# The up product of a batched LoRA kernel: float32 in 16-row, 64-column places of the array instead of float32r with split operands

## What is computed

```python
B_sel = B[adapter_ids]
A_sel = A[adapter_ids]
Bx = jnp.einsum('bni,bri->bnr', x, B_sel)
out = jnp.einsum('bnr,bor->bno', Bx, A_sel)
return x + out * SCALING
```

## Time and profile before

| | |
|---|---|
| median of 3 runs | 93.18 us (93.02 to 94.08) |
| profiled execution | 93.05 us |
| its span, first to last instruction | 91.3 us |
| TensorE busy | 79.9 us (88%) |
| VectorE, ScalarE, GpSimd busy | 59.6, 59.4, 64.1 us |
| DMA | 34.82 MB, mean 381 GB/s |
| granted TensorE clock, mean | 0.953 |

### The profile page before, as it was taken

The page is one execution under the profiler, slowest core; times in us unless marked ns, Lnnn a source line. Parts: engine busy times, 40 slices in busy tenths (PEclk is TensorE's granted clock), DMA queues, the critical chain, the costliest instruction groups (busy, mean ns, idle before and its releaser), DMA issues.

```text
span 91.3 us, 3632 instructions
## 1 busy us (share of the span) xinstructions
PE 79.9 (88%) x1466; PEld 63.2 (69%) x1466; DVE 59.6 (65%) x108; ACT 59.4 (65%) x155; POOL 64.1 (70%) x140
## 2 busy tenths in 40 slices
PE   3997899999999999999999999999999999563500
PEld 3996798877878778686878786878787877422100
DVE  0069541128695969696969696877768596998810
ACT  1356877996969596877869696969696959131000
POOL 6048955999897979797979788797979793810000
PEclk9999999999999999999999999999999999996555
DMA  0999999999999999999999999999999999989692
GB/s 20 314 381 413 406 408 413 404 408 413 400 408 413 400 409 409 406 406 404 409 417 404 417 417 409 415 413 411 417 413 411 417 413 415 386 321 377 275 384 88
DMA packets 10193, 34.82 MB, mean 381 GB/s; under 512 B 834, under 2 KB 1858, under 8 KB 10178
## 3 DMA queue, kind: packets, MB, share of 16 engines
q1 hardware_dynamic: 10032, 34.08, 93.8%
q10 hardware_dynamic: 146, 0.52, 1.5%
HBM read 17.83 MB, written 16.78 MB: 379 GB/s over the span
## 4 chain that ended last, share of the span: by engine, by line
PE 77%; DVE 6%; DMA 5%; ACT 2%; POOL 2%; DVEq 1%; issue 1%; POOLq 0%
PE t_bank L227 35%; PE bx_bank L238 19%; PE y_banks L258 19%; DMA x_all<-in_A 5%; PE y_banks L217 4%; DVE x_all L373 4%; POOL x_all L174 2%; DVE bx_parts L364 2%; DVEq L44 1%; ACT bx_parts L289 1%; ACT a_table L312 1%; ACT x_t L307 1%; DVE x_all L349 0%; POOLq L173 0%
## 5 line engine op out<-in xcount | busy, mean ns | idle before, releaser
L373 DVE TENSOR_TENSOR x_all<-y_banks,x_all 128x1024 f32<-128x1024 f32 x32 | 39.1, 1224 | 15.0 <-PE y_banks L258 14.5
L307 ACT COPY x_t<-t_bank 128x512 f32<-128x512 f32 x64 | 34.4, 590 | 12.1 <-PE t_bank L227 11.5
L166 POOL CAST a_duo<-a_table 128x512 fp32r x64 | 36.8, 617 | 3.7 <-ACT a_table L312 2.0
L227 PE MATMUL t_bank<-ident,x_all 128*128 128x128 f32 x256 | 34.9, 279 | 0.4 <-ACT x_t L307 0.4
L227 PEld LDWEIGHTS t_bank<-ident,x_all 128*128 128x128 f32 x256 | 27.5, 141 | 6.9 <-issue 5.3
L156 POOL COPY b_duo<-b_table 128x256 f32 x64 | 22.9, 403 | 7.8 <-PE bx_bank L238 7.8
L258 PE MATMUL y_banks<-a_duo,bx_parts 64*128 64x512 f32 x128 | 20.2, 434 | 3.3 <-ACT bx_parts L289 3.2
L238 PE MATMUL bx_bank<-x_t,b_duo 128*32 128x64 f32 x1024 | 20.7, 222 | 0.0
L238 PEld LDWEIGHTS bx_bank<-x_t,b_duo 128*32 128x32 f32 x1024 | 15.7, 109 | 5.4 <-issue 5.2
L364 DVE TENSOR_TENSOR bx_parts<-bx_bank,bx_parts 32x64 fp32r<-32x64 f32 x64 | 14.1, 220 | 4.8 <-ACT bx_parts L322 3.7
L258 PEld LDWEIGHTS y_banks<-a_duo,bx_parts 64*128 64x128 f32 x128 | 11.2, 192 | 7.0 <-issue 3.8
(11 more groups left out here) (12 smaller groups left out, 10.5 us busy)
## 6 DMA issues: line engine op xcount, KB each, us to landing
out_y<-x_all SPq DMA_DIRECT2D x32, 512.0 KB, 13.0
x_all<-in_x SPq DMA_DIRECT2D x15, 1024.0 KB, 19.1
x_all<-in_x SPq DMA_DIRECT2D x2, 512.0 KB, 6.1
x_all<-in_B ACTq DMA_DIRECT2D x1, 512.0 KB, 4.3
x_all<-in_A SPq DMA_DIRECT2D x2, 256.0 KB, 4.8
id_row<-in_ids ACTq DMA_DIRECT2D x1, 0.2 KB
```

Source lines behind the costliest of these rows:

```text
L166: last = nc.gpsimd.tensor_copy(a_duo[duo % 2][:, k, :], a_table[:, bass.ds(adapters[k] * BANK, BANK)])
L227: last = nc.tensor.transpose(t_bank[unit % 2][:, c * P:(c + 1) * P], x_all[:, 2 * duo + tile, at:at + P], ident[:, :])
L307: nc.scalar.copy(x_t[duo % 2][:, half * HALF:(half + 1) * HALF, tile, :], t_bank[unit % 2][:, :].rearrange("p (c n) -> p c n", c=HALF)).th ...
L373: nc.vector.tensor_tensor(here, product, here, ALU.add).then_inc(y_drained, 1)
```

## The change

- Up is float32, and nothing is split. Each of a duo's eight matmuls (two tiles, two sequences s, two halves h) has its own place: 16 rows in row group 2 x tile + h, 64 columns s. Nothing is accumulated: each writes its 64 tokens by 512 outputs alone.
- bx_bank's four quadrants hold a sequence's Bx each, 16 rows of 32. ScalarE copies them as they stand (128x64, L288), and each to the quadrant of the other half of the same tile (four copies of 16x64, L292). VectorE has no part in it, and does only the adds.
- B is gathered once (128 columns); A's table has each rank group at each quadrant.
- A is copied by VectorE alone, two copies of each group of adapters (L313), into a zeroed place; ScalarE's and GpSimd's parts in it go. VectorE copies six adapters to a_table, ScalarE two.
- Output halves are now even and odd columns pairs of a row of A (o as p, j, h), so the add steps through x by two.
- B's transposes go to bx_bank; transposes of x and of A are interleaved in another order at the start; 21 warm-up transposes.

```diff
-    A_BY_ACT = (1, 3, 5, 7)
-    A_BY_DVE = (0, 2, 4, 6)
-    WARM_UPS = 18
+    A_BY_ACT = (5, 7)
+    A_BY_DVE = (0, 1, 2, 3, 4, 6)
+    WARM_UPS = 21
...
-        b_duo = [sb(f"b_duo{i}", [P, DUO_SEQS, CHUNKS, QUAD]) for i in range(2)]
-        bx_parts = [sb(f"bx_parts{i}", [P, DUO_SEQS, P], F32R) for i in range(2)]
-        a_duo = [sb(f"a_duo{i}", [P, DUO_SEQS, BANK], F32R) for i in range(2)]
+        b_duo = [sb(f"b_duo{i}", [P, DUO_SEQS, CHUNKS, RANK]) for i in range(2)]
+        bx_sides = [sb(f"bx_sides{i}", [P, PER_TILE, SEQ]) for i in range(2)]
+        a_duo = [sb(f"a_duo{i}", [P, DUO_SEQS, BANK]) for i in range(2)]
...
-            for i in range(2):
-                nc.gpsimd.memset(bx_parts[i][:, :, :].bitcast(F32), 0.0).then_inc(parts_zeroed, 1)
+            nc.gpsimd.memset(a_copies[:, 0:GROUP, :, :], 0.0).then_inc(copies_zeroed, 1)
...
-                        last = nc.tensor.matmul(bx_bank[duo % 2][k * QUAD:(k + 1) * QUAD, 0:SEQ],
+                        last = nc.tensor.matmul(bx_bank[duo % 2][k * QUAD:k * QUAD + RANK, 0:SEQ],
...
-                            ranks = slice(h * K_UP, (h + 1) * K_UP)
-                            k = tile * PER_TILE + s
-                            last = nc.tensor.matmul(y_banks[tile][:, h * BANK:(h + 1) * BANK],
-                                                    bx_parts[duo % 2][ranks, k, :], a_duo[duo % 2][ranks, k, :],
-                                                    start=(s == 0), stop=(s == PER_TILE - 1))
+                            ranks = slice((2 * tile + h) * QUAD, (2 * tile + h) * QUAD + RANK)
+                            last = nc.tensor.matmul(y_banks[tile][s * SEQ:(s + 1) * SEQ, h * BANK:(h + 1) * BANK],
+                                                    bx_sides[duo % 2][ranks, int(s != h), :],
+                                                    a_duo[duo % 2][ranks, tile * PER_TILE + s, :],
+                                                    start=True, stop=True)
...
+                nc.scalar.copy(bx_sides[duo % 2][:, 0, :], bx_bank[duo % 2][:, 0:SEQ])
+                for tile in range(2):
+                    for s in range(PER_TILE):
+                        at, to = (2 * tile + s) * QUAD, (2 * tile + 1 - s) * QUAD
+                        last = nc.scalar.copy(bx_sides[duo % 2][to:to + RANK, 1, :],
+                                              bx_bank[duo % 2][at:at + RANK, 0:SEQ])
+                last.then_inc(bx_copied, 1)
...
+            nc.vector.memset(a_copies[:, GROUP:ADAPTERS, :, :], 0.0).then_inc(copies_zeroed, 1)
+            dve.wait_ge(copies_zeroed, 2)
             for g in range(2):
                 dve.wait_ge(a_loaded[g], 16)
-                for h in range(HALVES):
-                    nc.vector.tensor_copy(a_rounded(g, h, 0, 0), a_raw(g, h)).then_inc(a_high_dve, 1)
-                for h in range(HALVES):
-                    dve.wait_ge(a_high_dve, HALVES * g + h + 1)
-                    nc.vector.tensor_tensor(a_rounded(g, h, 0, 1), a_raw(g, h), a_part(g, h, 0, 0),
-                                            ALU.subtract).then_inc(a_rest_dve, 1)
+                for t in range(2):
+                    last = nc.vector.tensor_copy(a_copy(g, t), a_raw(g))
+                last.then_inc(a_copied, 1)
...
-                here = x_all[:, 2 * duo + tile, :].rearrange("n (p h j) -> n p h j", h=HALVES, j=J)
+                here = x_all[:, 2 * duo + tile, :].rearrange("n (p j h) -> n p h j", h=HALVES, j=J)
...
-            split_rest(0)
-            for duo in range(1, DUOS):
-                add_x(duo - 1, 0)
-                split_rest(duo)
-                add_x(duo - 1, 1)
-            add_x(DUOS - 1, 0)
-            add_x(DUOS - 1, 1)
+            for duo in range(DUOS):
+                for tile in range(2):
+                    add_x(duo, tile)
```

More of the change, by code:

```diff
@@ L9, in lora_kernel @@
 def lora_kernel(nc: bass.Bass, x: bass.AP, ids: bass.AP, a_in: bass.AP, b_in: bass.AP, out: bass.AP):
-    F32, F32R, I32 = mybir.dt.float32, mybir.dt.float32r, mybir.dt.int32
+    F32, I32 = mybir.dt.float32, mybir.dt.int32
     ALU = mybir.AluOpType
@@ L102, in a_bank, with a_raw, a_copy @@
             return y_banks[a % 2][:, half * BANK:(half + 1) * BANK]
[L104 to L111, removed]
+        def a_raw(g):
+            return (a_nat[:, g * GROUP:(g + 1) * GROUP, :]
+                    .rearrange("p a (j h r) -> p (a j) h r", h=HALVES, r=RANK))
+        def a_copy(g, t):
+            return (a_copies[:, g * GROUP:(g + 1) * GROUP, :, :]
+                    .rearrange("p a j (t h e r) -> p (a j) t h e r", t=2, h=HALVES, e=2)[:, :, t, :, 0, :])
         def a_row(a):
             return a_table[:, a * BANK:(a + 1) * BANK]
[L116 to L119, removed]
         @block.sync
@@ L198, in _ @@
                 for c in range(HALF):
-                    last = nc.tensor.transpose(t_bank[unit][:, c * P:(c + 1) * P],
+                    last = nc.tensor.transpose(bx_bank[unit][:, c * P:(c + 1) * P],
                                                b_nat[:, (unit * HALF + c) * P:(unit * HALF + c + 1) * P], ident[:, :])
@@ L223, in transpose_unit @@
                     pe.wait_ge(x_loaded[LOAD_OF[2 * duo + tile]], 16)
-                pe.wait_ge(t_copied, B_UNITS + UNITS * duo + unit - 1)
+                if duo or unit >= 2:
+                    pe.wait_ge(t_copied, B_UNITS + UNITS * duo + unit - 1)
                 for c in range(HALF):
@@ L264, in _ @@
                 a_unit(a)
[L265 to L268, removed]
+            transpose_unit(0, 0)
+            transpose_unit(0, 1)
+            a_unit(A_BANKS)
+            a_unit(A_BANKS + 1)
+            transpose_unit(0, 2)
+            transpose_unit(0, 3)
+            a_unit(A_BANKS + 2)
+            a_unit(A_BANKS + 3)
             for duo in range(DUOS):
@@ L311, in copy_a, with copy_bx @@
                 act.wait_ge(a_filled, a + 1)
-                nc.scalar.copy(a_row(a), a_bank(a)).then_inc(a_copied_act, 1)
-            def split_high(duo):
+                nc.scalar.copy(a_row(a), a_bank(a)).then_inc(a_table_act, 1)
+            def copy_bx(duo):
                 act.wait_ge(bx_done, duo + 1)
-                if duo < 2:
-                    act.wait_ge(parts_zeroed, duo + 1)
-                else:
+                if duo >= 2:
                     act.wait_ge(y_filled, 2 * (duo - 1))
-                for k in range(DUO_SEQS):
-                    s = k % PER_TILE
-                    last = nc.scalar.copy(bx_parts[duo % 2][0:QUAD, k, s * SEQ:(s + 1) * SEQ],
-                                          bx_bank[duo % 2][k * QUAD:(k + 1) * QUAD, 0:SEQ])
-                last.then_inc(high_done, 1)
@@ L342, in _ @@
[L342 removed]
+                    for unit in range(UNITS):
+                        copy_x(duo + 1, unit)
+                copy_bx(duo)
         @block.vector
         def _(dve):
+            nc.vector.memset(a_copies[:, GROUP:ADAPTERS, :, :], 0.0).then_inc(copies_zeroed, 1)
+            dve.wait_ge(copies_zeroed, 2)
             for g in range(2):
                 dve.wait_ge(a_loaded[g], 16)
[L348 to L353 removed]
+                for t in range(2):
+                    last = nc.vector.tensor_copy(a_copy(g, t), a_raw(g))
+                last.then_inc(a_copied, 1)
@@ L355, in _ @@
             for a in A_BY_DVE:
                 dve.wait_ge(a_filled, a + 1)
[L357 to L367 removed]
+                nc.vector.tensor_copy(a_row(a), a_bank(a)).then_inc(a_table_dve, 1)
```

102 lines of the change are left out of this document (28 added, 74 removed).

## The result

The changed kernel takes 94.81 us (median of 4 runs, 94.58 to 95.02) against 93.24 for the kernel before: ratio 1.018, 95% interval 1.015 to 1.020. It is slower, by more than the 1% that the prediction took as its bound; 91.0 was forecast, with a range of 89.8 to 94.8. Its profiled execution took 94.59 us for a span of 92.8.

The account below looks back on a forecast made before the run. TensorE and DMA were both read as nearly full, with compute setting the end. Span 91.3 us, -0.6 start, 0 periods, -2.0 end, +0.4 clock, +0.1 DMA: 89.2; with 1.75 around it, 91.0 us forecast, range 89.8 to 94.8.

Parts of the forecast that it names:

- TensorE waits for nothing: Mid-kernel chain before the change: TensorE alone, 4.32 to 4.34 us a duo, with no waiting.
- Up: Up in each duo: all eight float32 places run together, 1.12 us as before, bounds 1.05 and 1.35.
- Rivals 1, 2 and 3: Up slower: uneven starts 93.5 us (0.10); places partly blocked about 103 or 110 us (0.14); strict order 136 us (0.04).
- So the period stays 4.34 us.: Mid-kernel duos: copies and adds stay covered by TensorE, so 14 periods change the span by 0.
- rival 1: Up: places run but starts or weight loads are uneven, up 1.3 us, time 93.5 us; chance 0.10.
- Start and end: Loop begins 0.6 us earlier, near 13.1; at the end six adds take 7.5 us instead of 9.5, saving 2.0.
- a wait that I had ruled out: ScalarE's five small copies after down: 1.03 us, forecast as covered by some 0.5 us, so TensorE wouldn't wait.
- The floor: End of the span: remaining DMA traffic at 410 GB/s keeps the span from going under 88.4 us.
- Rival 4: End: stores fall behind and the DMA hides the gain, 91.5 us; chance 0.72 together with the forecast.

Follow-up runs that it names:

- runs 1 to 4: Changed kernel with 17 warm-up transposes and 2, 6, 12 or 18 small matmuls ahead of the work: 94.95, 95.37, 96.68 and 96.20 us.
- few_stores: Changed kernel storing only the first 128 of each tile's 1024 output columns: 90.66 us, ratio 0.975 to the kernel before.
- before_pad16: Kernel before with down's first four matmuls done twice in every duo, 192 instructions instead of 176: 97.54 us, ratio 1.050.
- down_half: Changed kernel with down over every second chunk only, 128 TensorE instructions in a duo instead of 192: 91.54 us, ratio 0.983 to the kernel before.
- s0: Changed kernel with 4 warm-up transposes fewer and 2 small float32 matmuls more ahead of the work: 94.95 us, ratio 1.021 to the kernel before.
- s16: As s0 but 6 small matmuls instead of 2, 16 instructions more ahead: 95.37 us, ratio 1.024 to the kernel before.
- s40: As s0 but 12 small matmuls instead of 2, 40 instructions more ahead: 96.68 us, ratio 1.035 to the kernel before.
- packets2k: Changed kernel with every load of x and every store cut into two of 2 KB per row: 97.71 us, ratio 1.050 to the kernel before.
- up_bf16: Changed kernel with up's operands (a_table, bx_sides, a_duo) in bfloat16, 176 instructions in a duo: 92.88 us, ratio 0.998 to the kernel before.
- s64: As s0 but 18 small matmuls instead of 2, 64 instructions more ahead: 96.20 us (93.55 to 97.22), too spread for a ratio.

## Why the prediction was wrong

**What bounded the kernel.** "TensorE waits for nothing" was read rightly from the earlier trace rows, but not how near it stood to a limit that no row of a busy engine shows. At 176 instructions a duo a block of 256 lasts 6.3 us, which is what the fetch needs under a full DMA. The kernel before was at its TensorE limit, within 2% of its DMA limit (91.3 against 89.8 us) and almost at its fetch limit together.

**Up.** Right in mechanism and size: 1.12 forecast, 1.04 measured. All eight places run at once: eight instructions start together, and the other eight 0.43 us later; that is 512 columns at two cycles, the price taken from the earlier trace rows. The second halves wait and the next places go on past them. The stops show that the program does have them product by product: before the one at 24.00 six products ran alone, with six starts and 0.45 us later six more, and behind it the other two did the same. The rule of strict program order (the Trainium skill, "TensorE: Matmul & The Clock Gate", packing small matmuls) would have given 4.1 us here; the trace doesn't agree with it. Rivals 1, 2 and 3 didn't happen.

**The failed step.** "So the period stays 4.34 us." I priced an operation by its time on the array, and never counted it as instructions, though I noted that a float32 product is two: up went from 16 to 32 instructions for each duo, all of TensorE's from 176 to 192. So the wait that I had at nothing, that for the program itself, cost 7.2 us: 4.1 in the stops and the split ups, 3.1 by the clock behind two of them. Undisturbed duos take 4.23 us, 0.11 less than forecast, worth 1.4 us over the 13 periods from the first up to the 14th; with the stops the mean period is 4.79. The stops are shown to be the fetch by three things: they keep their place in the program when the work is shifted (runs 1 to 4), go when the DMA is idle (few_stores), and appear in the old kernel at the new instruction count (before_pad16). That 94.81 lies so near the range's end is luck: its upper part stood for rival 1, an up of 1.3 us, which did not happen.

**Start and end.** The start was mis-sized. The 13.67 us of the earlier trace rows is the second duo's first transposes, where the loop begins in the program; the same transposes began at 12.01 us in the changed kernel, 1.7 us earlier, not 0.6 (13.1 forecast):

```profile
6.77 1.91 PE L192 MATMUL y_banks<-ident,x_all 128*128 128x128 f32 x16
...
12.01 1.04 PE L203 MATMUL t_bank<-ident,x_all 128*128 128x128 f32 x8
```

The 48 transposes from A on took the forecast 5.2 us, but A began at 6.77 instead of 7.9: B's eight took 1.04 us, not 1.91, since the clock had risen at 5.7 us (before, at 7.6). In the other runs of the changed kernel's kind it rose at 4.3 to 6.4 us, so part of this gain is that execution's luck. The adds after the 14th up took 7.6 us (7.5 forecast, 9.5 before): right. Behind them stand 3.15 us instead of 4.13. There was a wait that I had ruled out, once, ahead of 17.03 us: transposes of the third duo waited 0.2 us for ScalarE, which had the five copies ahead of theirs. Together the 14th up ends 5 us later than forecast (82.04 instead of 77.07): 7.2 from the late blocks and 0.2 from this wait, less 1.4 in the periods and 1.1 at the start.

**The floor.** The 88.4 us was too low: down_half's span is 89.8 us, though its sums end at 76.99. I let the DMA run at 410 GB/s up to its last packet, at 87.9 us, with half a microsecond behind it. In down_half the rate holds up to 85 us and then runs out slowly, at 334 and 37 GB/s in the last two slices; the last packet ends at 89.0 us, and 0.8 us follow. So by that run the most that this change could have brought is 93.1 - 91.5 = 1.6 us, and the forecast of 91.0 was out of reach even with every block in time. Rival 4 said that the DMA hides the gain, and had 91.5 us, but by another sum: a floor of 88.4 and a queue of stores.

**The clock.** In mid-kernel the granted clock fell to its lower level eight times in the traces of the changed kernel, s0, s16, s40, few_stores and packets2k, each time 0.8 to 2.3 us after TensorE had gone on from a stop of 1.35 to 1.7 us between two starts. Six of these stops stand inside up, two (at 61 us in the changed kernel and in s0) just ahead of it. Stops elsewhere, in down (1.38 us in s16 and s40) or just behind up (1.38 in s40, 2.4 in up_bf16), brought no fall, nor did up alone (down_half), nor the short stop at 43.7 us in the changed kernel. The spread runs of s64 don't fit: in its trace a stop of 1.36 us inside up brings none, and one of 1.75 us, with one matmul instruction of down left ahead of up, brings one. What makes the difference was not tested alone.

**No version beats both by much.** up_bf16 is 0.2% faster than the kernel before but drops half of the bits of up's operands. few_stores and down_half are faster only because they leave out output or half of the contraction. In full float32 I ran none with fewer instructions: down is 128 of the 192, and the ways I see of issuing fewer cost more TensorE time. That wasn't tried.

## What to carry to other kernels

Count TensorE's instructions as well as its time: weight load and matmul for each product, both twice in float32. Where the DMA is full, ask how long 256 of them last; here, under 6.3 us meant stops, which show as "issue" in the chain at a fixed number of instructions. Before pricing a saving in compute, find the DMA's floor by a run in which compute ends early, not by adding up its GB/s.

## What was not expected of the hardware

- TensorE's program comes in blocks of 16 KB (12 packets, 0.20 MB). Under a DMA of 410 GB/s a block began to move 2.2 to 4.4 us after the previous border had been crossed (1.6 to 2.1 in down_half), took about 1.0 us, and a stopped TensorE went on 2.2 to 2.7 us after it began: 6.3 us for 256 instructions (up_bf16).
- Eight float32 products, with 16 rows and 64 columns of weights and 512 columns streamed, each on its own place, take 1.04 us, where four float32r rounds took 1.12.
- A stop of 0.8 us in the midst of such a group costs 1.9 us (2.91 instead of 1.04), since the last four of its sixteen instructions then take 1.07 us by themselves.
- Rows of 2 KB instead of 4 KB moved 390 instead of 410 GB/s.
